# Attention on one core: where VectorE does the additions of the gathered expert rows

## What is computed

```python
qkv = xn @ w_qkv.T                       # 16 heads of 16
attn = q @ k.T / sqrt(16)                # |i - j| <= 128 is kept, the rest masked
out = softmax(attn) @ v                  # then @ w_proj.T
routed = sum over the 8 best of 64 experts of weight * expert(xn)
x = x + attention(xn) + shared(xn) + routed(xn)
```

## Time and profile before

| | |
|---|---|
| median of three runs | 1191.47 us |
| the profiled execution, time | 1188.81 us |
| its span | 1186.9 us |
| `attend`, from the first VectorE work to the last | about 751 to 1149 us |
| granted TensorE clock, mean of the span | 0.984 |

### The profile page before, as it was taken

The page is one execution under the profiler, slowest core; times in us unless marked ns, Lnnn a source line. Parts: engine busy times, 40 slices in busy tenths (PEclk is TensorE's granted clock), DMA queues, the critical chain, the costliest instruction groups (busy, mean ns, idle before and its releaser), DMA issues. The chain is left out here.

```text
span 1186.9 us, 36133 instructions
## 1 busy us (share of the span) xinstructions
PE 1102.7 (93%) x8352; PEld 809.3 (68%) x8353; DVE 792.1 (67%) x2511; ACT 770.5 (65%) x1900; POOL 631.5 (53%) x658
## 2 busy tenths in 40 slices
PE   6999799799999999999999988899999999999999
PEld 3445366499999999999999977445454555455457
DVE  6886698744545444544544534799999999999933
ACT  3555255478878778877787866366666666666653
POOL 0444203177666666666666644376666666666620
PEclk9999899999999999999999999799999999999999
DMA  6555300078888888888888998355656555655413
GB/s 220 160 154 162 111 8 21 11 227 272 258 239 245 246 246 242 248 246 238 255 246 249 248 176 179 100 148 139 161 154 165 140 154 154 169 142 145 137 58 121
DMA packets 138647, 207.54 MB, mean 175 GB/s; under 512 B 21217, under 2 KB 111329, under 8 KB 138594
## 3 DMA queue, kind: packets, MB, share of 16 engines
q1 hardware_dynamic: 110114, 120.10, 32.9%
q0 software_dynamic: 27648, 86.02, 29.3%
q10 hardware_dynamic: 832, 0.79, 0.3%
HBM read 243.26 MB, written 63.97 MB: 259 GB/s over the span
## 5 line engine op out<-in xcount | busy, mean ns | idle before, releaser
L991 POOL DMA_INDIRECT xb<-token_rows,idx_ring_x x320 | 303.2, 947 | 184.3 <-issue 144.2
L1022 PE MATMUL psum<-xTe,wgu 128*128 128x128 f32 x2560 | 341.1, 276 | 1.4 <-issue 0.8
L1609 POOL DMA_INDIRECT yg<-expert_rows,idx_ring x256 | 256.8, 1003 | 128.8 <-issue 47.6
L1022 PEld LDWEIGHTS psum<-xTe,wgu 128*128 128x128 f32 x2560 | 313.7, 193 | 2.3 <-ACT wgu L1074 1.3
L1439 ACT ACTIVATE pT<-psum 128x384 f32<-128x384 f32 (+1 forms) x512 | 214.7, 467 | 145.5 <-PE psum L1318 139.6
L1504 DVE CUSTOM_DVE_ANT_0 masked<-psum,mask_q 128x384 f32<-128x384 f32 (+1 forms) x512 | 245.3, 518 | 20.6 <-PE psum L1325 17.3
L1119 DVE TENSOR_SCALAR ys<-psum,xb 128x256 f32<-128x256 f32 x320 | 154.7, 484 | 129.9 <-PE psum L1032 103.9
L1074 ACT COPY wgu<-wb 128x512 f32 x320 | 197.9, 619 | 24.0 <-DMA wb<-in_w_exp 10.5
L1032 PE MATMUL psum<-wb,aT 128*128 x640 | 192.7, 383 | 8.5 <-DVE ys L1119 4.5
L1325 PE MATMUL psum<-qk 96*128 96x384 bf16 (+1 forms) x512 | 165.6, 326 | 25.9 <-DVE nmax L1504 11.3
L1110 DVE TENSOR_TENSOR aT<-gate,psum 128x128 f32<-128x128 f32 x320 | 92.0, 287 | 143.4 <-PE psum L1022 121.7
(11 more groups left out here) (136 smaller groups left out, 1136.6 us busy)
## 6 DMA issues: line engine op xcount, KB each, us to landing
wb<-in_w_exp SPq DMA_DIRECT2D x320, 384.0 KB
expert_rows<-ys SPq DMA_DIRECT2D x160, 256.0 KB
qk<-q_parts SPq DMA_DIRECT2D x64, 128.0 KB
qk<-k_parts SPq DMA_DIRECT2D x64, 128.0 KB
q_parts<-wb SPq DMA_DIRECT2D x32, 192.0 KB, 2.8
k_parts<-wb SPq DMA_DIRECT2D x28, 192.0 KB, 2.8
token_rows<-rows SPq DMA_DIRECT2D x8, 640.0 KB, 3.9
xb<-token_rows,idx_ring_x POOLq DMA_INDIRECT x320
```

What stands on the lines that cost most here:

```text
L991: nc.gpsimd.indirect_dma_start(out=xb[:, r, :], out_offset=None, in_=rows_d, in_offset=bass.IndirectOffsetOnAxis(ap=idx_ring[:, q, r:r + 1 ...
L1022: last = nc.tensor.matmul(banks[bank + r % 2][:, 0:P], wgu[:, r % NW, h, part * I:(part + 1) * I], xT[:, r % 2, h, :], start=(h == 0), sto ...
L1609: nc.gpsimd.indirect_dma_start(out=yg[:, h, k, :], out_offset=None, in_=y_d, in_offset=bass.IndirectOffsetOnAxis(ap=idx_ring[:, h, k:k + 1 ...
```

## The change

The table `SUMS` now lists by step what VectorE adds behind the four maxima of that step. In step 0 these are parts 0 and 1 of h = 0; in step 1 part 2; in step 2 part 3; part 4 goes between the reciprocal and the multiplication of `normalise` of step 3. Of h = 1, part 0 goes between the cast and the subtraction of `split_maxima` of step 4, part 1 behind step 5, part 2 behind step 6, part 3 between cast and subtraction of step 7, and part 4 behind it. Within a step the order is: maxima, split, sums, copy of turned maxima (step 0), normalise, copy of turned maxima (step 5). No instruction is added or taken away.

```diff
--- before.py
+++ after.py
@@ -1257,8 +1257,9 @@
-    SUMS = {(1, 0): (0, 0), (1, 2): (0, 1), (2, 0): (0, 2), (2, 1): (0, 3), (2, 3): (0, 4),
-            (5, 0): (1, 0), (5, 2): (1, 1), (6, 0): (1, 2), (6, 1): (1, 3), (6, 3): (1, 4)}
+
+    SUMS = ((0, 0), (0, 1)), ((0, 2),), ((0, 3),), (), (), ((1, 1),), ((1, 2),), ((1, 4),)
+    SUM_3, SUM_4, SUM_7 = ((0, 4),), ((1, 0),), ((1, 3),)
     def one_by_one(engine, group):
@@ -1506,13 +1507,15 @@
                                                mask_q[:, side:side + (hi - lo) * P], -1.0, -NEG, ALU.add, ALU.min,
                                                accum_out=nmax[:, hh, i:i + 1]).then_inc(s1_free, 1)
-            def split_maxima(g, part):
+            def split_maxima(g, part, between=()):
                 a, b = PARTS[part]
                 dve.wait_ge(s1_free, ahead_entry(g, b - 1, HG - 1) + 1)
                 high, low = (nmax_b[part][:, :, k, :] for k in range(2))
                 nc.vector.tensor_copy(high, nmax[:, :, a:b]).then_inc(hi_done, 1)
+                for sum_of in between:
+                    combine(g, *sum_of)
                 dve.wait_ge(hi_done, g * 2 + (part + 3))
                 nc.vector.tensor_tensor(low, nmax[:, :, a:b], high, ALU.subtract).then_inc(nmax_ready, 1)
@@ -1523,11 +1526,15 @@
                 nc.vector.tensor_copy(nmaxT[0:n, part, :], ring_bank(turn_entry(like(g), k)).bitcast(BF16)[0:n, 0:P]
                                       ).then_inc(s1_free, 1)
-            def normalise(of, half, g, k):
+            def normalise(of, half, g, k, between=()):
+
+
                 dve.wait_ge(s1_ready, turn_entry(g, k) + 1)
                 o = ring_bank(turn_entry(like(g), k)).rearrange("p (t h c) -> p t h c", t=HT, h=HG)
                 nc.vector.reciprocal(rec[:, half, :, :], o[:, :, :, DK]).then_inc(rec_ready, 1)
+                for sum_of in between:
+                    combine(g, *sum_of)
                 dve.wait_ge(rec_ready, of * 2 + (half + 1))
                 dst = onorm[:, half * HT:(half + 1) * HT, bass.ds(of, 1), :]
                 nc.vector.tensor_tensor(dst.rearrange("p t o (h d) -> p t (o h) d", h=HG), o[:, :, :, 0:DK],
@@ -1562,20 +1569,24 @@
                     for hh in range(HG):
                         if not is_last(g):
                             maxima(g, j, hh)
-                        if (j, hh) in SUMS:
-                            combine(g, *SUMS[j, hh])
+                    for at, part, between in ((CUT - 1, 0, SUM_4), (TT - 1, 1, SUM_7)):
+                        if j == at and not is_last(g):
+                            split_maxima(g, part, between)
+                        elif j == at:
+                            combine(g, *between[0])
+                    for sum_of in SUMS[j]:
+                        combine(g, *sum_of)
                     if j == TURN_AT[M_LATE]:
                         copy_maxima(g, 1, g, M_LATE)
                     if j == TURN_AT[O_0] and not is_first(g):
                         normalise(g - 1, 0, g, O_0)
-                    if j == TURN_AT[O_1] and not is_first(g):
-                        normalise(g - 1, 1, g, O_1)
-                    if j == 4 and not is_last(g):
-                        split_maxima(g, 0)
+                    if j == TURN_AT[O_1]:
+                        if is_first(g):
+                            combine(g, *SUM_3[0])
+                        else:
+                            normalise(g - 1, 1, g, O_1, SUM_3)
                     if j == TURN_AT[M_EARLY] and not is_last(g):
                         copy_maxima(g + 1, 0, g, M_EARLY)
-                    if j == 7 and not is_last(g):
-                        split_maxima(g, 1)
             for i in range(TT):
                 for hh in range(HG):
```

## The result

The changed kernel is 0.6% slower: 1198.58 us (median of seven runs, 1194.36 to 1201.30) against 1191.89 us of the kernel before in the same session, ratio 1.0061 with a 95% interval of 1.0045 to 1.0077. A later session gave 1197.59 against 1191.22 us, ratio 1.0053 (1.0029 to 1.0077). The forecast was 1184.8 us. The profiled execution of the changed kernel is the slowest of its seven (1201.30 us), and that of the kernel before one of its fastest (1188.81 us), so the profiles differ by 12.5 us where the medians differ by 6.7.

A forecast was written before the change was run, and what follows sets the result against it. VectorE and the ring were taken to pace steps 0 to 3, SyncE's chain steps 4 to 7. Gains of 5.2 (13 periods), about 1.0 (group 14) and 0.5 (group 0), 6.7 us, took 1191.5 to 1184.8 us; range 1178 to 1195.

The forecast's parts named there:

- steps 0 to 3: First half of an attention group, paced by VectorE and the ring: 11.6 us for 12.12, minus 0.5 us.
- TensorE's wait of 0.46 us for the multiplication of `normalise`: Step 3 of a group: a `scores_q` waited 0.46 us for VectorE; the wait was to go.
- VectorE does not wait for h = 1: Gathers of h = 1: the sum ends a microsecond earlier than needed, so no wait of VectorE.
- I take 9.25: GpSimd's refill of h = 0: first to last start of eight gathers 9.25 us, bounds 9.09 and 10.45.
- the loop of the gathers: Hold 9.8, to first gather 1.38, batch 9.25, landing 3.2: 23.6 us, bounds 23.0 and 24.8; as long as the period.
- a wait for the gathers of over 0.5 us: Sign of being wrong, VectorE before part 0 of h = 0: over 0.5 us means landing or batch was misjudged.
- slower: the gather loop decides: Rival, VectorE's wait at the end of step 0: loop from 24.0 us, at 24.8 gives 1202 us; chance 0.09.
- Taking VectorE out of the way in steps 4 to 7 can give nothing: Second half of groups 1 to 13: SyncE's loads and maxima DMAs set the pace, so gain taken as nothing.
- steps 4 to 7: Second half of a group: to stay as long as before, 11.88 us in the mean.
- the gain forecast for these groups (5.2 us): Groups 1 to 13: period 23.6 us for 24.00, 0.4 us in each of 13 periods.
- the forecast had 6.2 for these groups: Fourteen periods from group 1 to 15: 5.2 us from 13 periods and about 1.0 us from group 14's.

The follow-up runs named there:

- the run with h = 1 back: Changed kernel with the sums of h = 1 put back between the maxima of steps 5 and 6: 1198.18 us, ratio 1.0050.
- the control run: The changed kernel itself, unedited, run again in a later session: 1197.59 us, ratio 1.0053.
- the 17 executions above: Changed kernel unedited, two sessions: six with mean clock 0.966 to 0.970 took 1197.6 to 1204.1 us, five at 0.976 or more 1194.1 to 1197.6 us.
- the best version: Changed kernel with part 4 of h = 0 in step 2's normalise gap, k loads a step earlier, turned-maxima copy before the sums: 1177.62 us, ratio 0.9881.
- the four variants with one edit of the normal sessions: Changed kernel with part 4 of h = 0 behind step 2 (0.9962), h = 1 sums back (1.0050), k loads earlier (0.9994); kernel before with k loads earlier (0.9971).
- the last three kernels: Changed kernel with k loads earlier and part 4 of h = 0 behind step 2: 1184.04 us; in its normalise gap: 1180.78; plus copy first: 1177.62.
- the three variants that were made again: Changed kernel with part 4 of h = 0 behind step 2 (1186.73 us), h = 1 sums back between maxima (1198.18), or k loads earlier (1190.55).
- the run with the shorter hold: Changed kernel with part 4 of h = 0 behind step 2: 1186.73 us, ratio 0.9962; slow session 1444.48 us, ratio 1.0271.

## Why the prediction was wrong

**Right: steps 0 to 3.** Step 1 was to grow from 2.44 to 3.06 us and is 2.94; steps 2 and 3 were to fall from 3.70 and 3.89 to about 3.25 and are 3.22 and 3.14. TensorE's wait of 0.46 us for the multiplication of `normalise` is gone. VectorE does not wait for h = 1. The four steps take 11.3 us for the 11.6 forecast.

**The step that failed: "I take 9.25" for the batch, and with it the loop that sets the period.** The text said that the buffer's hold grows to 9.8 us and that the loop of the gathers becomes as long as the period, 23.6 us in every group. VectorE's and GpSimd's timelines of the changed kernel, a quiet group:

```profile
1044.80 1.32 DVE L1549 TENSOR_TENSOR yg<-yg 128x512 f32<-128x512 f32 x2
...
1054.38 0.42 DVE L1565 TENSOR_TENSOR res<-res,yg 128x256 f32 x1
```

```profile
1055.77 0.94 POOL L1620 DMA_INDIRECT yg<-expert_rows,idx_ring  x1 [3.17 <-DVE res L1565]
...
1064.52 0.95 POOL L1620 DMA_INDIRECT yg<-expert_rows,idx_ring  x1 [0.30 <-issue]
```

The hold is 9.58 us and the way to the first gather 1.39, as forecast, but the batch takes 8.75 us. With the 3.42 us to land of the run with h = 1 back the loop is 23.1 us, an estimate, and the period is 23.76: the loop does not bind there, and VectorE did not wait. In groups 7 and 14 the same batch takes 10.99 us and its landing 3.86 and 4.19 us, for the 3.2 forecast, so the loop is near 26 us. One number for the batch was too long in twelve groups, where it cost nothing, and 1.7 us too short in two, where everything waited. The batch is longer because one gap between two gathers is 3.20 us and not 1.25; why its landing is longer too is not known. The forecast's own sign of being wrong names the place, a wait for the gathers of over 0.5 us. The trace of before had the same two gaps, unused by the forecast. GpSimd's timeline of the kernel before:

```profile
922.31 0.94 POOL L1609 DMA_INDIRECT yg<-expert_rows,idx_ring  x1 [1.00 <-DVE res L1558]
925.51 0.94 POOL L1609 DMA_INDIRECT yg<-expert_rows,idx_ring  x1 [2.25 <-PE psum L1318]
...
1090.06 0.95 POOL L1609 DMA_INDIRECT yg<-expert_rows,idx_ring  x1 [1.00 <-DVE res L1558]
1093.26 0.94 POOL L1609 DMA_INDIRECT yg<-expert_rows,idx_ring  x1 [2.25 <-PE psum L1318]
```

They cost nothing there: the sum stood 6.04 and 6.27 us behind the start of the last gather of these batches, and the gathers need 3 to 4. In the changed kernel this slack is gone. The cost is 3.05 and 3.92 us on step 1 in the control run, and with what followed in step 2, part of it at the lower clock, 9.7 us of the 14 periods. The forecast's rival "slower: the gather loop decides" had the place and the sign, but wanted every batch to be long, and got 0.09.

**Not priced: what a wait in one piece does to the clock.** "Taking VectorE out of the way in steps 4 to 7 can give nothing" was booked as a zero, and it cost something. VectorE's stalls in steps 6 and 7 went (step 6 takes 2.66 us for 3.21), and the time came back as one wait of 1.2 to 2.2 us in front of step 0, in place of several of 0.2 to 0.6 us at other places. Behind it the clock was at 1.2 GHz for a part of steps 0 and 1 in six and in three groups of the two profiles, 7.2 and 3.2 us. In the kernel before, whose waits there are under 1 us, and in the run with h = 1 back, no step 0 shows it. That this fall is caused by the wait is argued from that and from the 17 executions above, not shown by an edit of its own; the same wait without the fall, at 1018.83, says that it is not the only condition.

**Hidden in the quiet group: the landing.** The period of a quiet group was forecast at 23.6 us and is 23.6 to 23.8, but that is luck in part: steps 0 to 3 were 0.3 us shorter than forecast, and steps 4 to 7, which were to stay as they were, took 12.44 us and not 11.88. Over groups 1 to 13 steps 4 to 7 take 12.35 us in the mean for 11.94 before, 5.3 us in all, as much as the gain forecast for these groups (5.2 us). SyncE's timeline of the changed kernel, against the earlier trace rows:

```profile
1061.47 2.68 SPq L1291 DMA_DIRECT2D qk<-nmaxT  x4
```

The queue is through at 1064.15 and TensorE starts at 1066.41: 2.26 us to land, for 1.59 before. In the mean of the thirteen groups it is 2.07 us (2.16 in the control run) for 1.74 before. The gathers of h = 0 now start 3.65 us later in the group and are on their way beside these DMAs, but that alone does not explain it: in the run with h = 1 back they start as late (1.80 us behind the start of step 4 in both), and the landing is 1.69 us. The cause stays open.

The sum of the control run comes out near the forecast again once both are taken off: 14 periods of 344.0 us, less 9.7 for late gathers and 3.2 for the clock, are 331.1, or 4.9 us under the kernel before; the forecast had 6.2 for these groups. The longer landing is still in the 331.1 us, and so is what steps 0 to 3 gave beyond the forecast.

## What to carry to other kernels

A buffer's loop (free, refill, land, use) has to be budgeted by its longest turn that the trace shows, not by its median; look through all the batches for the one odd gap before you spend the slack. Moving work off an engine does not shorten a fixed chain beside it: the waits come together in one place, and that can have a price of its own. And a forecast that comes out right in a quiet group should still be checked term by term, for two errors can cancel. Here the best version lets go of the buffer early and starts the fixed chain early; each alone was worth less.

## What the runs showed of the hardware

Between two indirect DMAs of GpSimd that wait for nothing, the distance was 1.25 us, but 3.20 us at two places of each profile of the kernel before and of the changed kernel, 112 gathers apart (922.31 to 925.51 and 1090.06 to 1093.26 in the kernel before). At the same counts the distance was 3.19 to 3.29 us in the four variants with one edit of the normal sessions, and 3.4 to 4.1 us in the last three kernels. What it is stays open: the second gather of a batch has no wait of its own in the code, and in the kernel before only gathers' own packets lie in that stretch.

TensorE's granted clock fell from 2.4 to 1.2 GHz in the middle of attention, where the engine is busy for 80% or more of every slice of the page. In groups 1 to 14 of six profiles (the kernel before, the changed kernel twice, and the three variants that were made again) each fall stands behind a wait of TensorE: all eight waits of 2.5 us or more were followed by one, and of those of 1.2 to 2.3 us some were and some were not (a fall behind 1.66 us in front of the step 0 at 993.86, none behind 2.22 us in front of the one at 1018.83).

And the whole kernel, in one session, ran at 1408 us instead of 1191, moving a fifth less per second in the expert stage (195 GB/s for 240). There the run with the shorter hold was 2.7% slower than the kernel before, and in the normal session 0.4% faster; the one with the loads of k earlier was 6.1% slower there, and the same here.
